# Order of the LoRA products, the mask products and the first loads in a conditional residual kernel

## What is computed

```
# layer 0: 8 experts, mixed by y, times one mask
w0[b] = sum_g y[b,g] * weight[g] * mask
x = x + einsum('bnt,bot->bno', x, w0) + bias0
# layer 1: a base matrix and 8 LoRA pairs of rank 16, weighted by y
out  = einsum('btc,oc->bto', x, W_base) + b_base
h    = einsum('btc,erc->bter', x, As)
lora = einsum('bter,eor,be->bto', h, Bs, y)
x = x + out + lora * 2.0
```

## Time and profile before

| | us |
|---|---|
| median of three runs | 57.01 (56.59 to 57.09) |
| the profiled execution, its time | 56.67 |
| its span | 54.9 |
| PE busy | 50.9 (93% of the span) |
| DVE, ACT, POOL busy | 39.4, 31.7, 31.7 |

### The profile page before, as it was taken

One profiled execution on the slowest core, in us unless ns is written; L12 is line 12 of the kernel. 1 busy time (PEld: TensorE's weight loads), 2 busy tenths in 40 slices (PEclk: granted clock), 3 DMA queues, 4 the chain that ended last, 5 costly groups with the idle time before them and its releaser, 6 DMA issues.

```text
span 54.9 us, 973 instructions
## 1 busy us (share of the span) xinstructions
PE 50.9 (93%) x330; PEld 45.6 (83%) x330; DVE 39.4 (72%) x64; ACT 31.7 (58%) x53; POOL 31.7 (58%) x30
## 2 busy tenths in 40 slices
PE   2998999999999999999999999999999999999900
PEld 2988889999998978998898889889889889888800
DVE  0049799939599996999999987689939809805030
ACT  1939950434719499629606992992992940850800
POOL 4001727099920099999994999999999910000000
PEclk9999999999999999999999999999999999999999
DMA  0699999999999997000720072063063054059582
GB/s 0 128 366 261 332 373 408 418 415 416 406 412 403 403 418 317 36 0 0 288 100 0 0 294 100 0 254 134 0 236 146 0 220 163 0 200 370 194 287 96
DMA packets 5476, 11.79 MB, mean 215 GB/s; under 512 B 608, under 2 KB 1376, under 8 KB 5472
## 3 DMA queue, kind: packets, MB, share of 16 engines
q1 hardware_dynamic: 5184, 11.35, 55.9%
q10 hardware_dynamic: 288, 0.39, 2.0%
HBM read 7.54 MB, written 4.19 MB: 214 GB/s over the span
## 4 chain that ended last, share of the span: by engine, by line
PE 87%; DMA 5%; ACT 1%; DVE 1%; issue 1%
PE ps_out L532 14%; PE ps_out L462 13%; PE ps_out L466 13%; PE ps_out L470 13%; PE ps_merge L462 7%; PE ps_merge L466 7%; PE ps_merge L470 7%; DMA lora_sb<-factors_B_dram 5%; PE ps_lora L476 3%; PE ps_lora L466 3%; PE ps_lora L462 3%; PE ps_lora L470 3%; ACT B_hi L232 1%; DVE out_sb L453 1%; PE ps_out L596 1%
## 5 line engine op out<-in xcount | busy, mean ns | idle before, releaser
L191 POOL TENSOR_TENSOR W_lo<-W,W_hi 128x512 fp32r<-128x512 f32 x8 | 13.2, 1652 | 2.2 <-ACT W_hi L240 2.2
L358 DVE TENSOR_TENSOR x_lo<-x_sb,x_hi 128x1024 fp32r<-128x1024 f32 x8 | 11.9, 1486 | 0.2 <-ACT x_hi L260 0.2
L462 PE MATMUL ps_out<-x_hi,M_hi 128*128 128x512 f32 (+1 forms) x32 | 9.8, 388 | 0.0
L466 PE MATMUL ps_out<-x_lo,M_hi 128*128 128x512 f32 (+1 forms) x32 | 9.7, 384 | 0.0
L470 PE MATMUL ps_out<-x_hi,M_lo 128*128 128x512 f32 (+1 forms) x32 | 9.7, 383 | 0.0
L253 ACT ACTIVATE M_hi<-ps_merge 128x512 fp32r<-128x512 f32 x8 | 4.8, 595 | 7.5 <-PE ps_merge L470 7.5
L197 POOL TENSOR_TENSOR W_lo<-W,W_hi 128x512 fp32r<-128x512 f32 x6 | 8.8, 1458 | 0.1
L201 POOL TENSOR_TENSOR W<-W,ident 128x256 f32<-128x256 f32 x6 | 6.5, 1093 | 3.7 <-DVE x_lo L358 3.7
L260 ACT ACTIVATE x_hi<-x_sb 128x1024 fp32r<-128x1024 f32 x8 | 8.4, 1056 | 0.0
L532 PE MATMUL ps_out<-packs_sb 128*128 128x128 f32 x64 | 8.2, 278 | 0.0
L373 DVE TENSOR_SCALAR out_sb<-ps_out,bias_sb 128x512 f32<-128x512 f32 x7 | 5.2, 746 | 4.1 <-PE ps_out L470 4.0
(11 more groups left out here) (58 smaller groups left out, 71.6 us busy)
## 6 DMA issues: line engine op xcount, KB each, us to landing
x_sb<-xT_dram SPq DMA_DIRECT2D x8, 512.0 KB, 10.8
outT_dram<-out_sb SPq DMA_DIRECT2D x15, 256.0 KB, 2.3
packs_sb<-packs_dram SPq DMA_DIRECT2D x7, 288.0 KB, 5.9
rows_sb<-rows_dram SPq DMA_DIRECT2D x1, 384.0 KB, 7.2
base_sb<-base_dram ACTq DMA_DIRECT2D x1, 256.0 KB, 3.9
outT_dram<-out_sb SPq DMA_DIRECT2D x2, 128.0 KB, 1.8
packs_sb<-head_dram SPq DMA_DIRECT2D x1, 192.0 KB, 3.8
packs_sb<-rest_dram SPq DMA_DIRECT2D x1, 160.0 KB, 4.9
```

What stands on the lines that cost most here:

```text
L191: pool.tensor_tensor(W1_lo[:, b % W1BUF], W1[:, b % W1BUF], W1_hi[:, b % W1BUF].bitcast(f32), ALU.subtract).then_inc(w1lo_done, 1)
L358: nc.vector.tensor_tensor(x_lo[:, b % XBUF], x_sb[:, b], x_hi[:, b % XBUF].bitcast(f32), ALU.subtract).then_inc(xlo_done, 1)
L462: nc.tensor.matmul(out, hi_l, hi_r, start=(n == 0), stop=False)
L466: nc.tensor.matmul(out, hi_l, lo_r, start=False, stop=False)
```

## The change

All six loads that the ramp needs now stand on SP's queue: B with the condition first (so the condition moves from A's tensor to B's), then A, head, rest and base; ACT issues none. PE runs the LoRA products of samples 0 to 3 ahead of all mask products, each into a bank of its own (the list ps_first: both ps_lora banks, then both ps_merge banks); the wait at L501 goes, and each first merge half gets a wait instead, until DVE has read the bank that it writes. In lora_first the A_hi product of sample 1 goes ahead of the A_lo product of sample 0. DVE makes six B_lo ahead of the first W1 add, and the W1 adds come earlier among the W0 multiplies. POOL makes three W1_lo ahead of the identity add eye_first, and the fourth right behind ramp_first. ACT makes W1_hi(2) ahead of W0_hi, and W1_hi(3) behind it. One warm-up matmul is dropped.

```diff
-    WARM = 28
+    WARM = 27
-    OB0, OB1, OA, OBT = NB, NB + NT, NB + 2 * NT, NB + 2 * NT + C
+    OBT, OB0, OB1, OA = NB, NB + C, NB + C + NT, NB + C + 2 * NT
...
+        ps_first = ps_lora + ps_merge
...
-            sp.dma_start(lora_sb[:, 0:OBT], factors_A).then_inc(lora_arrived, 16)
+            sp.dma_start(lora_sb[:, 0:OB0], factors_B).then_inc(B_arrived, 16)
+            sp.dma_start(lora_sb[:, OB0:OA + C], factors_A).then_inc(lora_arrived, 16)
             sp.dma_start(packs_sb[:, 0:cut], head).then_inc(mix_in, 16)
             sp.dma_start(packs_sb[:, cut:MIXW + PACKW], rest).then_inc(pack_in[0], 16)
+            sp.dma_start(base_sb[:, :, :], base.rearrange("p (j o) -> p j o", j=NT)).then_inc(base_in, 16)
...
             w1_lo(0)
+            w1_lo(1)
+            w1_lo(2)
             pool.wait_ge(w0_done, NQ // 2)
             pool.tensor_tensor(W0[:, 0:2, 0, 0:H], W0[:, 0:2, 0, 0:H], ident[:, :].unsqueeze(1).to_broadcast([P, 2, P]),
                                ALU.add).then_inc(eye_first, 1)
-            w1_lo(1)
             pool.wait_ge(ramp_hi, 1)
             pool.tensor_tensor(W0_lo[:, :, :, 0:H], W0[:, 0:2, :, 0:H], W0_hi[:, :, :, 0:H].bitcast(f32),
                                ALU.subtract).then_inc(ramp_first, 1)
-            w1_lo(2)
+            w1_lo(3)
...
-            act.dma_start(lora_sb[:, OBT:OBT + C], factors_B).then_inc(B_arrived, 16)
-            act.dma_start(base_sb[:, :, :], base.rearrange("p (j o) -> p j o", j=NT)).then_inc(base_in, 16)
             act.wait_ge(B_arrived, 16)
-            act.wait_ge(lora_arrived, 16)
...
             w1_hi(1)
+            w1_hi(2)
             act.wait_ge(eye_first, 1)
             nc.scalar.activation(W0_hi[:, 0:2, :, 0:H], W0[:, 0:2, :, 0:H], ACT.Copy).then_inc(ramp_hi, 1)
-            w1_hi(2)
+            w1_hi(3)
...
-                nc.vector.tensor_tensor(W1[:, b], ps_lora[b % 2][:, :, :], base_sb[:, :, :],
+                nc.vector.tensor_tensor(W1[:, b], ps_first[b][:, :, :], base_sb[:, :, :],
                                         ALU.add).then_inc(w1_done, 1)
...
             def lora(b):
                 pe.wait_ge(blo_done, b + 1)
-                pe.wait_ge(w1_done, b - 1)
...
             lora_first()
-            for q in range(4):
-                mixed(q)
             lora(2)
-            mixed(4)
-            mixed(5)
             lora(3)
-            mixed(6)
-            mixed(7)
+            for q in range(NQ):
+                mixed(q)
             for b in range(2):
                 pe.wait_ge(ramp_hi, 1)
                 pe.wait_ge(w1lo_done, b + 1)
+                pe.wait_ge(w1_done, b + 3)
                 merge_half(b, 0, (ramp_first, 1))
```

More of the change, by code:

```diff
@@ L59, in pack @@
                     packs_sb[:, at + EXPW:at + PACKW].rearrange("p (j t) -> p j t", j=NT))
-        lora_sb = sb("lora_sb", [P, OBT + C])
+        lora_sb = sb("lora_sb", [P, OA + C])
         cond_er = lora_sb[:, 0:NB]
@@ L219, in _ @@
             eye(4)
-            w1_lo(3)
             w0_lo(3)
@@ L295, in _ @@
                 nc.scalar.activation(W0_hi[:, b, :, H:C], W0[:, b, :, H:C], ACT.Copy).then_inc(ramp_hi, 1)
-            w1_hi(3)
             m_hi(0)
@@ L391, in _ @@
             dve.wait_ge(B_arrived, 16)
-            for b in range(4):
+            for b in range(6):
                 b_lo(b)
@@ L396, in _ @@
             w1(0)
-            b_lo(4)
-            b_lo(5)
+            w1(1)
             w0(0)
+            w1(2)
             w0(1)
-            w1(1)
             w0(2)
             w0(3)
+            w1(3)
             w0(4)
-            w1(2)
             w0(5)
             w0(6)
-            w1(3)
             w0(7)
@@ L481, in lora_first @@
                 term(0, 0, A_hi, B_hi, first=True)
+                pe.wait_ge(bhi_done, 2)
+                term(1, 0, A_hi, B_hi, first=True)
                 pe.wait_ge(alo_done, 1)
                 term(0, 0, A_lo, B_hi)
-                pe.wait_ge(bhi_done, 2)
-                term(1, 0, A_hi, B_hi, first=True)
                 term(1, 0, A_lo, B_hi)
@@ L500, in lora @@
                 pe.wait_ge(blo_done, b + 1)
-                pe.wait_ge(w1_done, b - 1)
                 for j in range(NT):
                     cols = slice(j * P, (j + 1) * P)
-                    mm = product(ps_lora[b % 2][:, j, :],
+                    mm = product(ps_first[b][:, j, :],
                                  [(A_hi[:, cols], A_lo[:, cols], B_hi[:, b], B_lo[:, b])])
@@ L574, in _ @@
             lora_first()
-            for q in range(4):
+            lora(2)
+            lora(3)
+            for q in range(NQ):
                 mixed(q)
-            lora(2)
-            mixed(4)
-            mixed(5)
-            lora(3)
-            mixed(6)
-            mixed(7)
             for b in range(2):
@@ L638 @@
     A_er = As.reshape(G * R, C)
-    lora = np.concatenate([np.repeat(cond.T, R, axis=0), halves(bias0[:, None]), halves(bias1[:, None]),
-                           A_er, Bs.transpose(0, 2, 1).reshape(G * R, C)], axis=1)
+    lora = np.concatenate([np.repeat(cond.T, R, axis=0), Bs.transpose(0, 2, 1).reshape(G * R, C),
+                           halves(bias0[:, None]), halves(bias1[:, None]), A_er], axis=1)
     rows = np.concatenate([halves(base), np.broadcast_to(bias0, (P, C))], axis=1)
@@ L647 @@
               "packs": packs[:, first:].reshape(P, NQ - 1, -1).transpose(1, 0, 2),
-              "factors_A": lora[:, :-C], "factors_B": lora[:, -C:], "base": halves(base.T), "rows": rows, "xT": xT}
+              "factors_A": lora[:, NB + C:], "factors_B": lora[:, :NB + C], "base": halves(base.T), "rows": rows, "xT": xT}
     arrays = {n: np.ascontiguousarray(a) for n, a in arrays.items()}
```

## The result

The changed kernel takes 57.38 us (median of four runs, 57.28 to 57.55); the kernel before, measured beside it, 56.80 (56.30 to 57.09). The ratio is 1.0154, with a 95% interval of 1.0089 to 1.0219: slower by about 1.5%. The time lies 0.18 us from the forecast and inside its range. The profiled execution has a span of 55.5 us against 54.9.

A forecast was written before the change was run, and what follows sets the result against it. PE bounds the kernel, so the start of lora_pair(4), held by base's landing through POOL's W0_lo, sets the end: +0.24 on 56.67 gives 56.91, or 57.25 by the median 57.01; forecast 57.2 us, range 56.5 to 58.0.

The forecast's parts named there:

- What bounds the kernel: After the first x product (19.46 us) PE works without a hole, untouched; the shift of lora_pair(4) carries to the end.
- From the W1 add to W0_lo: Ramp path over DVE, ACT and POOL: POOL's first W0_lo half (ramp_first) is done at t+7.91, forecast 15.67 us.
- t: Start of the first W1 add on DVE: 6.50 us before, forecast 7.76.
- t+8.94: Start of lora_pair(4) on PE when POOL's W0_lo decides: forecast 16.70 us, +0.24.
- What sets t: DVE's six B_lo (7.09 or 7.29) or base's landing + 1.36; base taken to land at 6.4 us.
- A in the second place of the queue: A, issued at 1.16 on SP, lands at 3.86 us; A_hi at 3.88, PE starts at 4.30, no gain.
- PE's own row: PE's lora and mask matmuls, reordered, let the merge begin at 14.45 instead of 14.95 us: 0.50 earlier.
- The clock costs nothing: One warm-up matmul less (0.11 us) lengthens PE's idle time before the first lora matmul, free while the clock holds.
- rival 3: Clock: half rate over PE's 24 lora matmuls adds 2.8 us, 1.2 hidden under POOL's wait; 58.9 us; chance 0.03.
- Rival 1: PE decides: base lands by 5.8, t is 7.15 or less; -0.3 to -0.5, 56.6 us; chance 0.25.
- rival 2: Base comes late behind head and rest, needing 4.9 us: t 8.83, +1.31, 58.3 us; chance 0.20.
- The other edits at nothing: Later ACT and DVE work, packs, bank waits, POOL's fourth W1_lo and the w1_done wait stay hidden: no cost.

The follow-up runs named there:

- base sixth: Changed kernel with base issued one place later on SP's queue, behind the first pack; 57.86 us, ratio 1.0231.
- rest on ACT's queue: Changed kernel with the load rest issued first on ACT's queue, base staying on SP, now fourth; 57.22 us, ratio 1.0101.
- base third: Changed kernel, all loads still on SP, but in the order B, A, base, head, rest; 56.46 us, ratio 0.9961.
- 28 warm-up matmuls: Changed kernel with the dropped warm-up matmul put back; 57.13 us, ratio 1.0131.
- the new loads alone: Kernel before, with its order of work, and only the new loads (B with the condition, A, head, rest, base, all on SP); 57.63 us, ratio 1.0204.
- POOL's other order: Changed kernel with POOL's third W1_lo moved behind W0_lo; 57.16 us, ratio 1.0129.

## Why the prediction was right or wrong

- *What bounds the kernel, and that only the start of the first x product matters.* Right: 35.44 us follow it before, 35.42 after.
- *From the W1 add to W0_lo.* The term t+7.91 was right to 0.03: 8.07 to 15.98 in the changed kernel, 8.76 to 16.64 with base sixth. lora_pair(4) came at t+9.02 (said: t+8.94).
- *What sets t.* The right cause, its size wrong, and this is the step that failed: base landed at 7.01, not at 6.4. I had bounds of 5.3 and 7.47 and took a value just below its own 3.9 us; it needed 4.4. Part of the 0.61 us came back in the next term: POOL's two adds took 0.88 us and not 1.19, since DVE had finished its B_lo and ran nothing beside them, so t was landing + 1.06. Together t was 8.07 against 7.76, and the start moved by 0.62 us instead of 0.24. That is the difference between "within 1%" and the measured 1.5%. That the time came out within 0.18 us of 57.2 is partly luck: I had added 0.24 to a kernel before of 57.01, and the one measured beside the change took 56.80, so that the medians differ by 0.58.
- *A in the second place of the queue.* Wrong by 0.5 us in the good direction: A_hi started at 3.38, not 3.88. A needed 2.7 us in the kernel before, with loads beside it on the other queue, and 2.2 here. PE began at 3.80, not at 4.30.
- *PE's own row.* Its work was right, its pace wrong: 14.45 foreseen for the merge, 15.13 measured in spite of the earlier start, because eleven lora matmuls ran at half rate (below), and because the 64 mask records stood 0.110 us apart and not 0.106, which is 0.27 of the 0.68 us. The hole at the merge was therefore 0.45 instead of 0.7 us long. In this execution it changed little, as POOL was later than PE.
- *"The clock costs nothing" and rival 3.* I had read the column of the granted clock, 1.00 in every slice, and said that no row at the lower level exists. There were rows: the warm-up matmuls of before, 28 in 3.17 us, or 0.11 us for 128 columns of bf16, which is the pace of 1.2 GHz (128/1.2 = 107 ns):

```profile
0.99 3.17 PE L573 MATMUL ps_merge<-warm 128*128 128x128 bf16 x28 [0.99 <-DVE warm L320]
```

  The rival's mechanism was real. It took 1 us of PE in the changed kernel's profile, under the wait for POOL, and 2 us in that of rest on ACT's queue, where all 24 lora matmuls ran at half rate and the execution took 58.77, near the 58.9 that I had for it. Whether the new order makes this likelier, one trace of each kernel can't tell.
- *Rivals 1 and 2.* Rival 1 is what base third gives (W1 add at 6.83, no hole), rival 2 in its mechanism is what happened, at half its price. I leaned on base's own 3.9 from a queue where only B stood ahead of it; as SP's fifth it needed 4.1 to 4.8 in the five profiles that have it there. The 4.9 of rest, on which rival 2 leaned, was no guide either: in the changed kernel rest needed 2.4. And that the bytes up to base are the same 870 KB said little: from 2 to 7 us DMA moved 255 GB/s in the changed kernel and 304 before.
- *The other edits at nothing.* Right in the profile of the changed kernel for the packs, the bank waits and the added w1_done wait: PE has no hole between 8.07 and 15.13. For the packs it does not hold in every execution: with 28 warm-up matmuls one came 0.85 us late. Incomplete for POOL's fourth W1_lo, which I placed in idle time: beside it DVE's identity add took 1.36 us, not 0.42. In the changed kernel that stayed hidden. In the two kernels with two W1_lo there, DVE's B_lo took 1.51 us as well, and PE waited.

Open: why DMA moves so little for one to two microseconds between 4 and 6 us (178 GB/s at the lowest in the kernel before, 114 in the changed one) and about 400 later. Nor is it shown that this makes base's 4.4 us: with the new loads alone the rate never fell below 247 in these 2 us, and base needed 4.8.

## What to carry to other kernels

A load's place in the queue is to be set by the time at which it is used and by how many engines hand its result on: base, needed at 6.5 us and followed by seven groups of steps on three engines, should not stand behind loads that are asked for at 8. When work is moved so that a late transfer gets covered, list which other transfer now has the least slack. And where the time between a load and PE runs over POOL, count POOL's instructions in the way as if they were PE's: three W1_lo where one stood took 0.9 of 1.3 us of slack (with base third W0_lo is done 0.32 us before its matmul), and base's later landing then made a wait of what was left.

## What the runs showed of the hardware

- **The clock column and the pace of matmuls disagree.** The busy table gives a granted clock of 1.00 in every stretch up to 20 us, yet in the changed kernel the 256-column matmuls start 0.21 us apart until 6.7 us and 0.12 apart from then on, which is the pace of 1.2 GHz and near that of 2.4 (256/1.2 = 213 ns, 256/2.4 = 107):

```profile
5.87 0.41 PE L474 MATMUL ps_lora<-B_hi,A_hi 128*128 128x256 f32 x1
...
6.08 0.41 PE L474 MATMUL ps_lora<-B_hi,A_lo 128*128 128x256 f32 x1
...
7.00 0.28 PE L460 MATMUL ps_merge<-B_hi,A_hi 128*128 128x256 f32 x1
...
7.12 0.29 PE L464 MATMUL ps_merge<-B_lo,A_hi 128*128 128x256 f32 x1
```

  The kernel with POOL's other order has the same PE row up to there, and in its profile the fast pace begins at 4.6:

```profile
4.79 0.28 PE L474 MATMUL ps_lora<-B_hi,A_hi 128*128 128x256 f32 x1
4.91 0.28 PE L474 MATMUL ps_lora<-B_hi,A_lo 128*128 128x256 f32 x1
```

  Its mask products begin at 7.05 and not at 8.07. So with the same PE row the moment differs between two executions by 2 us, worth 1 us of PE. In the thirteen profiles it lies between 4.3 us or earlier (before) and about 9.8 (rest on ACT's queue). It is latest in the two where PE stood 0.90 and 0.46 us for A ahead of its first lora product, 8.3 and 9.8. That the spread of the runs of one kernel (before: 56.06 to 57.55 in 17) comes from this is possible, but was not shown. The Trainium skill, "TensorE: Matmul & The Clock Gate", "The HAM clock gate", says that the throttled state is the default, that activity releases it, and that the moment varies from run to run. These rows agree, the clock column doesn't. The page gives half a microsecond either way for the variation; the two kernels above lie 2 us apart.
- **Loads on two queues take from each other.** B and A landed 2.0 to 2.2 us after their issue in eight of the nine profiles in which SP's queue was alone (in the ninth A took 2.8), and 2.6 to 3.3 in the four with loads on ACT's queue beside them. That agrees with the section of the Trainium skill that I weighed ("DMA: Bandwidth & Descriptors", "Issuing engines are not separate DMA queues"): loads from all issuing engines run on the same DMA engines and interleave. That a second issuing engine saves nothing beyond issue time, as it also says, these runs neither show nor refute: from 2 to 7 us three of the four kernels with two queues moved more than any with one (304 to 328 GB/s against 240 to 285).
- **POOL and DVE slow each other.** DVE's B_lo took 0.48 us alone and 1.51 beside POOL's subtraction, in three kernels; its identity add 0.42 alone and 0.77 to 1.36 beside it; POOL's two adds to base 0.86 to 0.92 alone, 1.05 to 1.36 beside DVE's B_lo.
